# Cross-attention of a decoder layer: TensorE takes the value products of two steps together, behind the first maxima of every second step, and VectorE adds the bias behind that maximum

## The reference, cut to what matters

```python
q = (query @ Wq.T + bq) * d ** (-0.5)          # b=4, sq=1024, h=16 heads, d=16
k = key_ @ Wk.T + bk                           # sk=154
v = value @ Wv.T + bv
scores = jnp.einsum('bhqd,bhkd->bhqk', q, k)
distance_bias = -jnp.log(distances + 1e-09) * jnp.abs(distance_scaling)
scores = scores + distance_bias[:, None, :, :]
attn = jax.nn.softmax(scores, axis=-1)
out = jnp.einsum('bhqk,bhkd->bhqd', attn, v)
```

## Time and profile before

| | |
|---|---|
| median of 3 runs | 3001.93 us (2994.0 to 3009.13) |
| profiled execution, its own time | 3001.78 us |
| its span in the trace | 3000.1 us |
| span of `attend_cross` after its first eight units | 2036.06 to 2349.7 us |
| TensorE busy over the whole span | 91% |

### The profile page before, as it was taken

One profiled execution on the slowest core, in us unless ns is written; L12 is line 12 of the kernel. 1 busy time (PEld: TensorE's weight loads), 2 busy tenths in 40 slices (PEclk: granted clock), 3 DMA queues, 4 the chain that ended last, 5 costly groups with the idle time before them and its releaser, 6 DMA issues. The chain is left out here.

```text
span 3000.1 us, 43235 instructions
## 1 busy us (share of the span) xinstructions
PE 2734.7 (91%) x14144; PEld 1804.3 (60%) x14145; DVE 2057.8 (69%) x3577; ACT 1407.2 (47%) x2556; POOL 977.3 (33%) x1000
## 2 busy tenths in 40 slices
PE   7989999999999899999998999758999589999995
PEld 6755555555555345555554555446666469788895
DVE  4568888888887488778877887445665558333337
ACT  2315666666667444444444545323444343333334
POOL 4557540000000164333435554451000450334322
PEclk9988999999999899999999999978999799999998
DMA  6999986545360354554554552264655423322425
GB/s 221 317 254 274 244 233 81 69 60 77 52 82 16 78 133 140 152 166 144 147 164 130 142 138 90 86 158 83 111 104 93 133 94 114 136 87 104 175 85 169
DMA packets 246194, 400.04 MB, mean 133 GB/s; under 512 B 37711, under 2 KB 147895, under 8 KB 244727
## 3 DMA queue, kind: packets, MB, share of 16 engines
q1 hardware_dynamic: 177940, 251.20, 31.5%
q10 hardware_dynamic: 49299, 82.70, 13.0%
q0 software_dynamic: 18768, 63.79, 6.9%
HBM read 231.46 MB, written 166.14 MB: 133 GB/s over the span
## 5 line engine op out<-in xcount | busy, mean ns | idle before, releaser
L655 DVE TENSOR_REDUCE an_m<-an_psm 128x1 f32<-128x512 f32 x1024 | 627.1, 682 | 102.6 <-PE an_psm L580 101.9
L634 ACT ACTIVATE an_probs<-an_pst 128x512 f32<-128x512 f32 x1024 | 521.7, 624 | 281.4 <-PE an_pst L608 281.4
L1411 ACT ACTIVATE wj_probs<-wj_pst 128x512 f32<-128x512 f32 x512 | 297.8, 595 | 354.2 <-PE wj_pst L1253 350.7
L1128 POOL TENSOR_TENSOR wj_sums<-wj_sums,wj_probs 128x512 f32<-128x512 f32 x192 | 265.5, 1383 | 320.5 <-ACT wj_probs L1411 317.5
L1442 DVE TENSOR_REDUCE wj_m<-wj_pm 128x1 f32<-128x512 f32 x512 | 324.0, 680 | 16.9 <-PE wj_pm L1228 16.6
L608 PE MATMUL an_pst<-an_qs,an_ks 128*128 128x512 f32 x640 | 265.0, 414 | 8.4 <-ACT an_probs L634 5.0
L580 PE MATMUL an_psm<-an_ks,an_qs 127*128 127x512 f32 x640 | 257.5, 402 | 1.8 <-DVE an_m L655 1.8
L1242 PE MATMUL wj_pacc<-wj_probs,wj_vs 128*64 128x512 f32 x1024 | 250.1, 609 | 2.7 <-ACT wj_probs L1411 2.7
L1253 PE MATMUL wj_pst<-wj_qs,wj_ks 128*128 128x512 f32 x512 | 203.8, 398 | 0.0
L1128 DVE TENSOR_TENSOR wj_sums<-wj_sums,wj_probs 128x512 f32<-128x512 f32 x192 | 180.4, 939 | 20.2 <-ACT wj_probs L1411 20.2
L1168 POOL MEMSET wj_qs<- 64x2048 f32 x2 | 3.5, 1800 | 576.5 <-issue 576.5
(11 more groups left out here) (432 smaller groups left out, 6025.3 us busy)
## 6 DMA issues: line engine op xcount, KB each, us to landing
ew_w<-scr_ws SPq DMA_DIRECT2D x10, 3072.0 KB, 11.5
scr_ws<-wide_pair POOLq DMA_DIRECT2D x27, 1024.0 KB, 5.5
ac_qs<-scr_xq ACTq DMA_DIRECT2D x48, 256.0 KB, 5.2
an_qs<-scr_q SPq DMA_DIRECT2D x40, 256.0 KB, 10.6
an_ks<-scr_k SPq DMA_DIRECT2D x40, 256.0 KB, 13.1
wj_qs<-scr_mq ACTq DMA_DIRECT2D x18, 512.0 KB, 5.0
wj_ks<-scr_mk ACTq DMA_DIRECT2D x18, 512.0 KB, 6.2
scr_xs<-x_acc SPq DMA_DIRECT2D x2, 4128.0 KB, 15.9
```

The lines of the kernel that those rows point to most:

```text
L634: act.activation(probs[:, (NSTEP * G + s) % HELD, j], pst[:, (GH * s + j) % RING], ACT.Exp, scale=HD ** -0.5).then_inc(exp_done, 1)
L655: dve.tensor_reduce(m1[:, hq, kh, col:col + 1], psm[:, part % MB], AX.X, ALU.max).then_inc(mx_done, 1)
L1128: eng.tensor_tensor(sums[:, x % CPB, j], earlier, probs[:, s % RING, j], ALU.add).then_inc(sum_done[j], 1)
L1411: act.activation(probs[:, x % RING, j], pst[:, j], ACT.Exp, scale=BHD ** -0.5).then_inc(exp_done, 1)
```

## The change

In an even step TensorE takes the values of both steps before it, one after the other, between its two units, and in an odd step none. The last two steps' values stand at the end. VectorE takes, in an even step, the first reduction ahead of the addition, not behind it. In the last group there are no units.

```diff
@@ block.tensor @@
                     if G + 1 < NGRP:
                         unit(G + 1, PER * s)
-                    if s > 0:
-                        values(G, s - 1)
-                    elif G > 0:
-                        values(G - 1, NSTEP - 1)
+                    if e == 0 and NSTEP * G + s > 0:
+                        for done in (NSTEP * G + s - 2, NSTEP * G + s - 1):
+                            values(done // NSTEP, done % NSTEP)
                     if G + 1 < NGRP:
                         unit(G + 1, PER * s + 1)
+            values(NGRP - 1, NSTEP - 2)
             values(NGRP - 1, NSTEP - 1)
@@ block.vector @@
                     qh, e = divmod(s, 2)
                     done = NSTEP * G + s
+                    if e == 0 and G + 1 < NGRP:
+                        unit(G + 1, PER * s)
                     dve.wait_ge(plain_ready, done + 1)
...
                     if G + 1 < NGRP:
-                        for n in range(PER * s, PER * s + PER):
+                        for n in range(PER * s + (e == 0), PER * s + PER):
                             unit(G + 1, n)
```

## The result

The changed kernel takes 3020.81 us (median of 14 runs, 3015.17 to 3028.26) against 3003.25 us (14 runs, 2994.0 to 3012.27) before: ratio 1.0052, 95% interval 1.0039 to 1.0065. The change makes the kernel half a per cent slower: by the ratio some 16 us (12 to 20), by the two medians 17.6. The profiled execution took 3022.04 us; its span is 3020.3.

The account below looks back on a forecast made before the run. The prediction took TensorE's own sequence in `attend_cross` to set the pace. Its terms, 23.2 + 1.5 - 2.0 - 12 - 4 = +6.7 us on 3001.78, gave 3008.5 us; range 2996 to 3020, the forecast's own 3004 to 3016.

Parts of the forecast that it names:

- rival (a): Row of maxima in `attend_cross` lands no earlier, only 6.5 us of waits saved: +14.7 us, 3016.5 to 3018; chance 0.24.
- The pair, +0.80: Odd step keeps its length, even step's second set of values adds 0.80 us; 29 pairs give +23.2 us.
- The addition behind the first maximum costs nothing: VectorE's moved addition in even steps ends 0.27 us before the next step's plain scores need it: no cost.
- Rival (c): VectorE's addition in even steps comes late, 0.3 us per pair over 29 pairs: +9 us, 3017; chance 0.06.
- Late second units, -2.0: Two even steps whose second unit started late after a batch's reciprocals get 1.1 us shorter each: -2.0 us.
- The last group, +1.5: Without units, odd steps wait for the addition and exponential, last values stand together: 14.6 to 16.1 us, +1.5.
- The row waits, -12: TensorE's nine waits for the row of maxima, 17.7 us: mid-group ones mostly go, group-start ones shrink by 0.80 each: -12 us.
- The clock, -4: TensorE's clock falls only behind long row waits; two of three gone or short gives -4 us (0 to -6.3).
- Rival (d): TensorE's clock falls in odd steps, idle 0.9 us each: 1.5 us in 29 pairs, +44 us, 3045; chance 0.03.

Follow-up runs that it names:

- after_fill: The changed kernel with the odd step's first unit put between the two heads of the biased scores; ratio 1.0009 to the kernel before, stage 310.1 us.
- pe_only: The kernel before with TensorE's half of the change alone, values in pairs and VectorE's order as before; ratio 1.012, stage 350.2 us.
- dve_only: The kernel before with VectorE's half of the change alone, TensorE's values one set per step; ratio 0.9987, stage 307.5 us.
- after_bal: The changed kernel with 192 KB of loads moved out of each group's first odd step; ratio 1.0096 to the kernel before, stage 329.1 us.
- fill_notail: after_fill with single values per step in the last group, except two sets in its step 0; ratio 1.0017 to the kernel before, stage 306.8 us.

## Why the prediction was right or wrong

The forecast was no difference that could be told, +6.7 us, with 3008.5. The measured median, 3020.81, lies 12 us above it and 0.8 above the range's end of 3020. By the ratio, on the first median of before, it is 3017.5: inside the range, outside the forecast's own bounds (3004 to 3016), and where rival (a) had been put (3016.5 to 3018). The direction of the sum was right; the likeliest case was not what came.

- **The pair, +0.80.** 5.32 + 4.44 - 8.94 = +0.82. Right in both parts: the odd step keeps its length with 0.89 idle, the second set of values costs 0.86. after_fill shows that the idle part is the cost: with the gap filled a pair takes 9.07, +0.13.
- **The addition behind the first maximum costs nothing.** Right, with 0.2 us to spare (forecast 0.27) while there are units. Rival (c) did not come. pe_only gives the edit's worth, 26 us.
- **Late second units, -2.0.** Right: the two steps that took 5.6 in all three traces of before, 1.1 more than others, take 5.4 like their neighbours.
- **The last group, +1.5.** It was +2.5 (17.7 against 15.2, last copy included), beyond the bound of +2: undersized. TensorE waited twice 0.56 us for the addition there and once 0.39 for the exponential.
- **The row waits, -12.** This is the step that failed. Beyond the usual 4.47 and 4.45 of an odd step, waits lengthened the steps ahead of them by 17.5 us on average over the three traces of before and by 8.3 in the two of the changed kernel: -9.2. For the middle of a group the mechanism was right and the term too small: 12.7 us on average, and all of it went (forecast 8.5), as the second leg now leaves ahead of the loads. For the group's start I wrote that "those loads keep their distance, and these waits only shrink by 0.80 each". They grew: from 7.1, 4.8 and 2.6 us in the traces of before to 8.5 and 8.2, so +3.5 where -3.5 was forecast, and what had been a few long waits became one in each group.

  The term looked at the loads ahead of the first leg, those of the odd step. The ones that decide are the even step's own, which its second leg stands behind. SP's queue and ScalarE's before, in the even step that began at 2164.49:

```profile
2168.29 0.31 ACTq L1823 DMA_DIRECT2D bias_keys<-scr_xk  x1
...
2170.46 0.57 SPq L1842 DMA_DIRECT2D ac_qs<-scr_xm  x1
...
2173.22 0.34 SPq L1850 DMA_DIRECT2D scr_xcraw<-ac_ev  x1
```

  Here the row landed 8.73 us into the step, 4.9 behind the issue of the first load and 0.3 behind the landing of the second, 256 KB, at 8.42. In the changed kernel (2203.17 to 2208.51) it was 5.3 behind the issue. In the five traces of the two kernels, 49 rows for a group's start had their second leg leave between 0.2 and 2.5 us behind that load (about half of such rows before, nearly all after). They landed 4.7 to 5.6 us after the load was issued, 5.1 on average, however early they had left themselves. So the row comes with the loads.

  Before, the loads left 3.9 us into the step and such a row was there at about 8.9, due at 8.94. Now they leave at 5.2 and the row is there at about 10.4, due at 9.77: 0.6 us late, 14 times, which makes the 8.3. dve_only has the loads at 4.8 and the row due at 9.3: by the same sum 0.7 late, and its 14 steps grew by 0.7 each.

  The first leg, too, runs beside more traffic, as the loads of the even step before now leave 1.4 us later. The DMA engines' share from 2 to 4 us into such a step is 0.53 on average before and 0.82 after (here 0.48 and 0.73; columns as in the earlier trace rows),

```profile
2166.49:2168.49 2.00, 2.00 (x17) 1.08 (x16) 1.40 (x2) 1.93 (x3) 0.00 (x0) 1.00 0.48 58
```

```profile
2199.96:2201.96 2.00, 2.00 (x23) 1.00 (x21) 0.94 (x2) 0.14 (x1) 0.00 (x0) 1.00 0.73 119
```

  the first row before, the second after. But that is the smaller part: from issue to landing the first leg took 4.5 us on average before and 4.8 after, the second 3.0 and 4.1. after_bal, where the second leg gets ahead of the loads, has one wait.
- **The clock, -4.** It was -3. It still falls, in two steps of each trace of the changed kernel, where the prediction had once at most. In the first trace they took 6.97 instead of 5.40, at group starts after waits of 0.63 and 0.45, so "only behind the long waits" does not hold either; before, such steps cost 4.7 to 7.2 us per trace. Rival (d) did not come: with 0.89 us idle in each pair the granted clock is 0.98 over the stretch, against 0.97 before, and in pe_only, which idles in even and odd steps, it is 1.00. (d)'s 3045 also left out the forecast's +6.7, which (c)'s 3017 has; it should have been 3052.

Together: 29 x 0.82 = 23.8, first steps +0.3, late units -2.3, waits -9.2, clock -3.0, last group +2.5, and 0.06 at each waiting step +0.4: +12.5, the 12.5 of the stage. That the ratio still fell into the range is in part luck: the range was wide enough to take in a term of which one half had the wrong sign. Rival (a)'s time came out, but not by its mechanism: the rows of one kind did land earlier.

The whole kernel lost 15.6 (12 to 20), 3 more than the stage, and that part stays open. The stage began at 2036.1 to 2041.4 in the three traces of before and at 2042.7 to 2051.6 in the eleven of edited kernels, in code that is the same. The last reduction of the self-attention already began at 962.5 to 970.0 before and at 967.9 to 973.4 in the others. All eleven stages began later than all three of before, by 6 us on average. If the edits had no part in it, such an order would come by chance once in 364 times, so it may be more than scatter; no run here tests what it is. Scatter between executions also bears on the combined versions: fill_notail's profiled execution took 3000.72 us, near its fastest run (2997.75, median 3006.55), so its stage of 306.8 is no mean.

Of the Trainium skill's two statements in "DMA: Bandwidth & Descriptors", section "Queues, rings and completion order", the traces agree with the second, that an increment lands only behind every earlier write of its engine, across queues: the second leg took 3.3 to 4.8 us in the first trace of the changed kernel, behind 320 KB, and 2.1 where the DMA engines' share was 0.03, and it came with the loads, however early it had left. No run here separates it from plain sharing of the engines.

## What to carry to other kernels

Work that stands between two uses of a single buffer is cover for the other engine's turn. Gathering it in every second place saved 0.14 us per pair here and bared a wait of 0.89 us in the place left empty: before moving it, ask what fills that place. And when a queue's issue time moves, follow each small transfer that runs against it, leg by leg; one may get ahead of the bulk loads while the other lands with them, later by as much as they are. A single trace of a kernel whose waits vary is a poor base for a term of 10 us: three traces of the same kernel gave 307.6 to 313.6.

## What was not expected of the hardware

Two sets of 32-column products behind one another cost 1.86 us, one alone 1.00. If the second set costs 0.86, about 0.14 of the first are spent in going from full-width products to 32-column ones and back; this is an estimate from the two numbers, and no run looks at the passage itself.

The step that began at 2269.08 in the changed kernel ran at the low clock behind a wait of only 0.45 us, while the waits of 0.66 (changed) and 1.99 (before) brought no such step:

```profile
2269.08 1.13 PE L1936 MATMUL ac_pst<-ac_qs,bias_keys 128*128 128x512 f32 x2 [0.45 <-DMA ac_qs<-scr_xm]
...
2273.39 1.92 PE L1948 MATMUL ac_pacc<-ac_probs,ac_vs 128*32 128x512 f32 x16
2276.05 0.67 PE L1936 MATMUL ac_pst<-ac_qs,bias_keys 128*128 128x512 f32 x2
```

The granted clock over its first 1.9 us (the last number but two; columns as in the earlier trace rows):

```profile
2269.08:2271.00 1.92, 1.92 (x5) 1.55 (x6) 0.78 (x3) 0.00 (x0) 0.00 (x0) 0.53 0.40 138
```

The first record is 1.13 long instead of 0.73, and the granted clock is 0.53, so nearly all of these 1.9 us ran at the lower of its two levels, 0.5. From 2273.39 to 2276.05, where the values take their usual 1.92, it is 1.00. Every group start of the changed kernel has the same two idle stretches ahead of it (0.89 and then the row), and only two of 14 fell, one at 2166.32 and this; what tells these from the others no run here shows.
